# Gates of pairs 0 and 1 ahead of the branch, gelu low halves with routing between them, later w2 halves, block gathers at other places

## The chip, the cores and the metric

One core of a Trainium2 chip runs the whole program in one launch. The metric is the device time of that launch in microseconds. The kernel before was timed three times: 191.04, 191.51 and 192.29 us, median 191.51.

## The reference, cut to what matters

A small language-model tower on 4 x 512 tokens, width 128:

```python
h = take(W.T, x, axis=0)                              # token rows
n = layernorm(h)
s_t = tanh(s_{t-1} @ A.T + n_t @ B.T)                 # recurrence over 512 positions
y = einsum('bth,oh->bto', s, C)
h = h + (sigmoid(y @ Wg.T + bg) * y) @ Wo.T + bo
m = layernorm(h); logits = m @ gate_w.T               # top 1 of 8 experts, its weight is 1
moe = (silu(m @ w1[e].T) * (m @ w3[e].T)) @ w2[e].T   # e: the token's own expert
h = h + moe + gelu(m @ sw1.T) @ sw2.T                 # inner width 512
```

## The kernel before, in words

Tokens are 16 tiles of 128 rows. Five engine programs are written out by hand in order; semaphores alone order one engine against another. An engine never passes its own waiting instruction.

*Recurrence.* The 512 positions of 4 sequences are cut into 32 chunks of 16, and all chunks are run together as 128 columns: 40 warm-up steps and 16 real ones, `STEPS` = 56. Step i is two matmuls on PE (L457 input part, L459 state part, banks 0 and 1 by turns) and one tanh on ACT (L670). Beside it the tiles are gathered, normalised and turned (`turn_pair`, L444; `bring`, L663), and the weights are prepared: every f32 weight matrix is split into a scaled f16 high half and an f16 low half. ACT squares w3 and w2 pieces for their maxima (L680), PE turns and spreads the maxima (L466, L469 at `MAX_STEPS` and two steps behind), DVE makes powers of two of them, and from `HIGH_STEP` on ACT writes one high half of w3 or w2 per step (L690, L692). DVE writes the low halves (L920 for w1, L935 for w3 and w2; 512 columns each for the latter).

*Branch.* Five steps before the end DVE compares warmed-up states with those of the neighbouring chunk (L958 to L964) and writes `agree_i`. PE and ACT load it into a register and branch: if the chunks do not agree, the recurrence is done again position by position; on this data that body is skipped.

*Attention pairs.* A pair is two tiles, 256 columns of the last 16 steps' states. For pair n PE does gate(n) = wgc x states (L500) and c(n) (L520), ACT a tanh (L713), DVE `gated` (L975), PE wo (L529), DVE `attn_out` (L982), statistics and `shift`, POOL a power for the variance (L383), ACT `norm2` (L740), PE turns it (L538), ACT and DVE write its f16 halves `x_ffn` (L733, L999), and PE computes the logits (L545). All gates use bank 2, so gate(n) waits for tanh(n-1).

*Gelu stage.* The shared expert has 16 pieces n (4 groups of 4 tiles, times 4 slices of the inner width). PE `up(n)` (L510, 3 matmuls of 512 columns) into one of four banks; ACT gelu (L720), then the high half one piece behind (L725, function `shared`); DVE the low half (L1005, `act_low_half(n)`, semaphore `act_low`); `up(n)` waits for low half n-4. `down(m)` (L564, 12 matmuls of 128 columns) needs all four low halves of its group; after four of them DVE adds the group to `attn_out` (L1083, `take_down(g)`, semaphore `base_ready`), and SP stores it (L341). down of groups 2 and 3 waits for `base_ready` of the group two before. Between its low halves DVE computes the routing: counts, places, slots, one-hot lanes (L1060), and PE inverts the permutation with 16 small matmuls (L587) after down(`INVERT_AT`). DVE makes row indices of it (L1065 to L1076).

*Blocks.* Tokens are worked through in blocks of 128 rows of one expert, 20 on this data. POOL gathers a block's rows from `x_rows` (L395, `take_block(k)`), PE turns it (L600), ACT and DVE write its halves (L751, L1096 `turned_low`), PE w1 and w3 (L621), ACT silu (L760), DVE product (L1112), PE turns it (L634), halves (L767, L1125), PE w2 (L646), DVE output (L1120, L1138), POOL adds the rows to `out` in DRAM (L402). The first `AHEAD` = 13 gathers are written out ahead of the first add; the rest come between the adds.

## Time and profile before

| | |
|---|---|
| timed runs | 191.04, 191.51, 192.29 us |
| the profiled execution's own time | 191.32 us |
| its span in the trace | 189.5 us |
| busy: PE, DVE, ACT, POOL | 142.1, 129.6, 104.1, 81.1 us |
| mean granted clock of PE | 0.958 of full |

The span runs from the first to the last instruction in the trace; the profiled execution's time has 1.8 us more around it. A row of the timeline is a start, a duration, the engine, the line and the operation, with the tiles it writes and reads; in brackets stands how long the engine was idle before, and who released it. "issue" there means that the engine waited for nothing that the profile shows. A tile `w_sb` stands for several weight buffers, which are reused late in the program for other data (gelu low halves, gathered blocks, silu and products); `states` likewise holds the gelu high halves in the end. Line numbers are those of the kernel before.

### The profile page before, as it was taken

What the parts mean: (1) busy time and instruction counts of PE and PEld (TensorE: products, weight loads), DVE (VectorE), ACT (ScalarE), POOL (GpSimd) and SP (SyncE); (2) the same over time, 40 slices, a digit from 0 to 9 for tenths busy, and PEclk for the clock granted to TensorE, in tenths of its full rate; (3) what the DMA queues carried; (4) which work ended last, traced back from release to release, by engine and by line L of the source; (5) the groups of instructions that cost most, each with busy time, mean ns of one, the idle gap of its engine ahead of it and who ended that gap; (6) DMA issues with size and microseconds to landing.
All of it is one profiled execution on the core that took longest, in us unless ns stands there. A gap on an engine that the chain in (4) does not pass through costs nothing.

```text
span 189.5 us, 3241 instructions
## 1 busy us (share of the span) xinstructions
PE 142.1 (75%) x1001; PEld 100.7 (53%) x1001; DVE 129.6 (68%) x363; ACT 104.1 (55%) x239; POOL 81.1 (43%) x77
## 2 busy tenths in 40 slices
PE   0107977788888879886776986869999999999720
PEld 0106855566656557664324654854776666676510
DVE  0245767849778886898689782434878788887720
ACT  2002433799449973685997672317666566565400
POOL 4777855600000000334000076134488888887580
PEclk9999999999999999999697899699999999999995
DMA  5563346992000000111100013041023234343331
GB/s 150 176 180 99 108 143 195 338 386 103 0 0 0 3 0 3 40 74 55 55 3 0 0 42 109 5 166 58 28 37 53 31 44 43 39 37 40 28 31 14
DMA packets 9955, 13.83 MB, mean 73 GB/s; under 512 B 1936, under 2 KB 4752, under 8 KB 9936
## 3 DMA queue, kind: packets, MB, share of 16 engines
q1 hardware_dynamic: 5904, 9.91, 15.6%
q0 software_dynamic: 4032, 3.67, 12.4%
q8 instruction: 11, 0.18, 0.4%
q14 instruction: 8, 0.07, 0.1%
HBM read 10.17 MB, written 3.41 MB: 72 GB/s over the span
## 4 chain that ended last, share of the span: by engine, by line
PE 41%; ACT 18%; POOL 11%; DVE 10%; issue 9%; DMA 6%; SPq 1%; POOLq 0%; ACTq 0%; DVEq 0%
PE bank L621 13%; POOL emb_rows L351 8%; PE bank L646 7%; PE bank L564 7%; ACT attn_out L680 5%; PE bank L634 4%; PE bank L510 3%; ACT states L670 3%; DMA w_sb<-w 3%; ACT w_hl L690 3%; PE bank L459 2%; DMA emb_rows<-emb,tok_sb 2%; ACT bank L720 2%; ACT w_hl L692 2%; ACT states L725 2%
## 5 line engine op out<-in xcount | busy, mean ns | idle before, releaser
L402 POOL DMA_INDIRECT out<-out_blk,row_of x20 | 31.4, 1570 | 9.8 <-DVE out_blk L1138 5.6
L459 PE MATMUL bank<-states,sq_sb 128*128 128x128 f32 x112 | 27.3, 326 | 5.9 <-ACT states L670 1.0
L621 PE MATMUL bank<-w_hl,xblk_t 128*128 x120 | 29.2, 379 | 0.8 <-issue 0.8
L383 POOL TENSOR_TENSOR rstd<-vareps,cst 128x2 f32<-128x2 f32 x8 | 5.6, 697 | 47.8 <-DVE vareps L799 47.8
L459 PEld LDWEIGHTS bank<-states,sq_sb 128*128 128x128 f32 x112 | 17.4, 196 | 14.2 <-ACT states L670 13.4
L457 PE MATMUL bank<-x_in,sq_sb 128*128 128x128 f32 x112 | 23.4, 291 | 1.3 <-issue 0.7
L670 ACT ACTIVATE states<-bank 128x128 f32<-128x128 f32 x56 | 15.5, 276 | 13.4 <-PE bank L459 10.3
L395 POOL DMA_INDIRECT w_sb<-x_rows,row_in x16 | 15.4, 961 | 14.3 <-PE bank L600 7.2
L760 ACT ACTIVATE w_sb<-bank,factor 128x512 f32<-128x512 f32 x20 | 13.8, 688 | 13.4 <-PE bank L621 13.3
L457 PEld LDWEIGHTS bank<-x_in,sq_sb 128*128 128x128 f32 x112 | 17.9, 201 | 2.7 <-issue 1.9
L1112 DVE SCALAR_TENSOR_TENSOR w_sb<-bank,factor,w_sb 128x512 f32<-128x512 f32 x20 | 15.0, 749 | 5.9 <-ACT w_sb L760 4.7
L351 POOL DMA_INDIRECT emb_rows<-emb,tok_sb x16 | 15.6, 972 | 6.5 <-issue 4.3
L646 PE MATMUL bank<-w_hl,w_sb 128*128 x160 | 16.6, 246 | 2.2 <-DVE out_blk L1138 2.1
L510 PE MATMUL bank<-x_ffn,sw_hl 128*128 128x512 f16 x48 | 15.2, 438 | 3.7 <-DVE w_sb L1005 3.6
L621 PEld LDWEIGHTS bank<-w_hl,xblk_t 128*128 128x128 f16 x120 | 11.3, 98 | 11.3 <-issue 1.6
L1005 DVE SCALAR_TENSOR_TENSOR w_sb<-bank,factor,states 128x512 f16<-128x512 f32 x16 | 11.7, 744 | 7.1 <-ACT states L725 3.7
L564 PE MATMUL bank<-sw_hl,states 128*128 128x128 f16 x128 | 14.4, 240 | 2.0 <-issue 2.0
L720 ACT ACTIVATE bank<-bank,factor 128x512 f32<-128x512 f32 x16 | 10.7, 675 | 8.5 <-PE bank L510 6.7
L646 PEld LDWEIGHTS bank<-w_hl,w_sb 128*128 128x128 f16 x160 | 12.6, 98 | 4.3 <-issue 3.1
L767 ACT ACTIVATE w_sb<-bank 128x512 f16<-128x512 f32 x20 | 11.9, 597 | 4.1 <-PE bank L634 3.3
L1125 DVE TENSOR_TENSOR w_sb<-bank,w_sb 128x512 f16<-128x512 f32 x20 | 13.6, 681 | 0.5 <-ACT w_sb L767 0.5
L564 PEld LDWEIGHTS bank<-sw_hl,states 128*128 128x128 f16 x128 | 11.8, 110 | 3.7 <-issue 2.3
(144 smaller groups left out, 276.6 us busy)
## 6 DMA issues: line engine op xcount, KB each, us to landing
w_sb<-w SPq DMA_DIRECT2D x24, 256.0 KB, 6.1
x_rows<-norm SPq DMA_DIRECT2D x4, 256.0 KB, 2.4
out<-attn_out SPq DMA_DIRECT2D x4, 256.0 KB
sw_sb<-sw SPq DMA_DIRECT2D x2, 256.0 KB
cst<-consts SPq DMA_DIRECT2D x1, 420.0 KB
sq_sb<-sq SPq DMA_DIRECT2D x1, 384.0 KB
out<-out_blk,row_of POOLq DMA_INDIRECT x20
emb_rows<-emb,tok_sb POOLq DMA_INDIRECT x16
```

What stands on the lines that cost most here:

```text
L351: pool.indirect_dma_start(out=emb_rows[:, t, :], out_offset=None, in_=emb, in_offset=bass.IndirectOffsetOnAxis(ap=tok_sb[:, t:t + 1], axis=0),
L395: pool.indirect_dma_start(out=xblk(k), out_offset=None, in_=x_rows, in_offset=bass.IndirectOffsetOnAxis(ap=row_in[:, k:k + 1], axis=0),).t ...
L402: pool.indirect_dma_start(out=out, out_offset=bass.IndirectOffsetOnAxis(ap=row_of[:, k:k + 1], axis=0), in_=out_blk[k % RING][:], in_offse ...
L457: pe.matmul(by_batch(pre), bt, x_at[:, p, :, PADK - shift:XB - shift], start=True, stop=False)
L459: pe.matmul(pre, at, states[:, i * COLS:(i + 1) * COLS], start=False, stop=True).then_inc(pre_ready, 1)
L510: mm = pe.matmul(ups[n % UPS][:], sw1_hl[:, a, i * P:(i + 1) * P], x_ffn[:, b, g * GC:(g + 1) * GC], start=(j == 0), stop=(j == 2))
L564: mm = pe.matmul(bank[2 + g % 2][:, t * P:(t + 1) * P], (act_hi, act_lo)[a][:, g, i, t * P:(t + 1) * P], sw2_hl[:, b, i * P:(i + 1) * P], ...
L621: mm = pe.matmul(hb[:], xblk_t[:, k % 3, b * P:(b + 1) * P], w[:, bass.ds(e * INNER + a * EXPERTS * INNER, INNER)], start=(j == 0), stop=( ...
L646: mm = pe.matmul(bank[6][:, 0:width], (prod_hi, prod_lo)[a][:, u, i * P:(i + 1) * P], w[:, bass.ds(at_i, width)], start=(i == 0 and a == 0 ...
L670: act.activation(states[:, (i + 1) * COLS:(i + 2) * COLS], bank[i % 2][:, 0:COLS], ACT.Tanh).then_inc(state_ready, 1)
L720: act.activation(ups[n % UPS][:], ups[n % UPS][:], ACT.Gelu, scale=gelu_in).then_inc(gelu_done, 1)
L1112: dve.scalar_tensor_tensor(out=prod[:, u, :], in0=bank[2 + u][:], scalar=prod_scale, in1=silu[:, u, :], op0=ALU.mult, op1=ALU.mult).then_i ...
```

## The change

- `TURN_AT`: pairs 6 and 7 are turned after steps 11 and 13, before after 10 and 12. The second spread matmul moves from step 34 to 36 (`SPREAD_STEPS`), the high halves begin at step 38 instead of 39. The w1 high half is written in two pieces, the second behind the maxima; the low halves of w1 are cut 2, 2, 4 instead of 3, 3, 2.
- Gate(0) goes into the recurrence after step 53, gate(1) after step 54, in banks 2 and 3; their tanh follow tanh 54 on ACT, ahead of the branch. Step 55, the last, is moved behind the branch, and on PE behind c(0). If the branch is taken, the two gates are done again in it.
- Three of DVE's five w2 low halves that stood ahead of the pairs move behind `take_down(1)`, `(2)` and `(3)`. PE waits for the last of them (`w_split` 3) only before the first w2 matmuls.
- In the gelu stage DVE's low halves stand earlier among the routing; `take_down(0)` stands before low half 13; the inverse follows down(6), before down(2).
- POOL's gathers: 0 and 1 at once, 2 and 3 behind the last low half, 4 and 5 behind `base_ready` 2 and 3, 6 to 12 behind turned blocks 1, 2, 2, 3, 4, 4, 5. Before, 0 to 3 at once, 4 to 7 behind low halves 9, 11, 13, 15, and 8 to 12 behind turned blocks 1 to 5.

```diff
+TURN_AT = {0: 1, 2: 2, 4: 3, 6: 4, 8: 5, 11: 6, 13: 7}
+SPREAD_STEPS = (22, 36)
-HIGH_STEP = 39
+HIGH_STEP = 38
-INVERT_AT = 2
+TURNED_FIRST = (1, 2, 2, 3, 4, 4, 5)
+INVERT_AT = 6
+        gate_bank = lambda n: bank[3 if n == 1 else 2]
...
             for k in range(AHEAD):
-                if BESIDE <= k < BESIDE + 4:
-                    pool.wait_ge(act_low, 9 + 2 * (k - BESIDE))
-                elif k >= BESIDE + 4:
-                    pool.wait_ge(blk_turned, k - BESIDE - 3)
+                if k == 2:
+                    pool.wait_ge(act_low, GROUPS * IC)
+                elif k in (4, 5):
+                    pool.wait_ge(base_ready, k - 2)
+                elif k >= 6:
+                    pool.wait_ge(blk_turned, TURNED_FIRST[k - 6])
                 take_block(k)
...
+            def gate(n):
+                if n >= 2:
+                    pe.wait_ge(tanh_ready, n)
+                pe.matmul(gate_bank(n)[:, 0:PC], wgc[:], kept(n), start=True, stop=True).then_inc(wg_done, 1)
-                    if i == at_step + 2:
+                    if i == spread_step:
                         pe.wait_ge(diag_ready, b + 1)
...
                 if i == STEPS - 3:
                     pe.wait_ge(close_ready, 1)
-                    pe.transpose(bank[2][0:1, 0:P], close_row[:, 0:1], ident).then_inc(close_turned, 1)
+                    pe.transpose(bank[7][0:1, 0:P], close_row[:, 0:1], ident).then_inc(close_turned, 1)
+                    pe.wait_ge(wgc_ready, 1)
+                    gate(0)
                 if i == STEPS - 2:
+                    gate(1)
                     pe.wait_ge(agree_ready, 1)
...
-            gate(0)
             for s in range(PAIRS + 5):
                 if s < PAIRS:
                     n = s
+                    if n == 1:
+                        advance(STEPS - 1)
+                        pe.wait_ge(state_ready, 1 + STEPS)
+                        pe.wait_ge(sh_split, 3)
...
-                if s + 1 < PAIRS:
+                if 1 <= s and s + 1 < PAIRS:
                     gate(s + 1)
...
                 if i == STEPS - 2:
+                    act.wait_ge(bg_ready, 1)
+                    gate(0)
+                    gate(1)
                     act.wait_ge(agree_ready, 1)
...
+            advance(STEPS - 1)
...
-            for j in range(EXPERTS - 5, EXPERTS):
-                w2_low(j)
+            w2_low(EXPERTS - 5)
+            w2_low(EXPERTS - 4)
...
             for g in range(1, GROUPS):
                 take_down(g)
+                w2_low(EXPERTS - GROUPS + g)
```

PE at the branch, before: the end of step 53 and the first instructions of the pairs, with the body of the branch between them left out. L457 and L459 are a step, L473 turns the row of agreements, L476 loads the register.

```order
L459 MATMUL bank<-states,sq_sb 128x128 [waits state_ready]
L473 MATMUL bank<-cst,close_row 1x128 [waits close_ready]
L457 MATMUL bank<-x_in,sq_sb 128x128
L459 MATMUL bank<-states,sq_sb 128x128 [waits state_ready]
L476 TENSOR_LOAD agree_i [waits agree_ready]
L476 ISA x2
L457 MATMUL bank<-x_in,sq_sb 128x128
L459 MATMUL bank<-states,sq_sb 128x128 [waits state_ready]
L479 COMPARE_AND_BRANCH
```

Here the load stands between steps 54 and 55. The first after the branch, also before:

```order
L500 MATMUL bank<-states,wgc 128x256 [waits state_ready,sh_split,wgc_ready]
L520 MATMUL bank<-states,sq_sb 128x256
L500 MATMUL bank<-states,wgc 128x256 [waits tanh_ready]
L520 MATMUL bank<-states,sq_sb 128x256
L500 MATMUL bank<-states,wgc 128x256 [waits tanh_ready]
```

Gate(0) opens the pairs there. The same two places now (L465 and L467 are a step, L475 a gate, L492 the row of agreements, L498 the load, L538 c(n)):

```order
L467 MATMUL bank<-states,sq_sb 128x128 [waits state_ready]
L492 MATMUL bank<-cst,close_row 1x128 [waits close_ready]
L475 MATMUL bank<-states,wgc 128x256 [waits wgc_ready]
L465 MATMUL bank<-x_in,sq_sb 128x128
L467 MATMUL bank<-states,sq_sb 128x128 [waits state_ready]
L475 MATMUL bank<-states,wgc 128x256
L498 TENSOR_LOAD agree_i [waits agree_ready]
L498 ISA x2
L501 COMPARE_AND_BRANCH
```

Two gates stand in front of the load, and no step behind it. After the branch, on PE too:

```order
L538 MATMUL bank<-states,sq_sb 128x256 [waits state_ready]
L465 MATMUL bank<-x_in,sq_sb 128x128
L467 MATMUL bank<-states,sq_sb 128x128 [waits state_ready]
L538 MATMUL bank<-states,sq_sb 128x256 [waits sh_split,state_ready]
L475 MATMUL bank<-states,wgc 128x256 [waits tanh_ready]
```

Step 55 stands behind c(0), and gate(2) is the first gate left.

DVE in the second half of the gelu stage, before. L1005 is a low half, L1060 a half of the one-hot lanes, L1065 to L1076 the indices, L1083 `take_down`.

```order
L1060 TENSOR_TENSOR w_sb<-late,lane_i 128x1024
L1005 SCALAR_TENSOR_TENSOR w_sb<-bank,factor,states 128x512 [waits act_high]
L1060 TENSOR_TENSOR w_sb<-late,lane_i 128x1024
L1005 SCALAR_TENSOR_TENSOR w_sb<-bank,factor,states 128x512 [waits act_high]
L1065 TENSOR_SCALAR row_in<-bank 128x23 [waits inverse_done]
```

Low halves 6 and 7 stand beside the lanes, the indices follow. Behind the indices, on DVE before:

```order
L1005 SCALAR_TENSOR_TENSOR w_sb<-bank,factor,states 128x512 [waits act_high] x4
L1083 SCALAR_TENSOR_TENSOR attn_out<-bank,factor,attn_out 128x512 [waits down_done]
L1005 SCALAR_TENSOR_TENSOR w_sb<-bank,factor,states 128x512 [waits act_high] x4
L1083 SCALAR_TENSOR_TENSOR attn_out<-bank,factor,attn_out 128x512 [waits down_done] x3
L1096 TENSOR_TENSOR xblk_t<-bank,xblk_t 128x128 [waits xt_high] x2
```

Eight low halves are left there, three `take_down` in a row behind them.

Now (L1037 a low half, L1104 lanes, L1046 `take_down`, L967 a w2 low half, L1132 `turned_low`):

```order
L1104 TENSOR_TENSOR w_sb<-late,lane_i 128x1024
L1037 SCALAR_TENSOR_TENSOR w_sb<-bank,factor,states 128x512 [waits act_high] x2
L1104 TENSOR_TENSOR w_sb<-late,lane_i 128x1024
L1037 SCALAR_TENSOR_TENSOR w_sb<-bank,factor,states 128x512 [waits act_high] x2
L1046 SCALAR_TENSOR_TENSOR attn_out<-bank,factor,attn_out 128x512 [waits down_done]
L1037 SCALAR_TENSOR_TENSOR w_sb<-bank,factor,states 128x512 [waits act_high]
L1112 TENSOR_SCALAR row_in<-bank 128x23 [waits inverse_done]
```

Five low halves and `take_down(0)` have come in front of the indices. Behind the indices, now:

```order
L1037 SCALAR_TENSOR_TENSOR w_sb<-bank,factor,states 128x512 [waits act_high] x2
L1046 SCALAR_TENSOR_TENSOR attn_out<-bank,factor,attn_out 128x512 [waits down_done]
L967 SCALAR_TENSOR_TENSOR w_hl<-w_sb,scale_i,w_hl 128x4x128 [waits w_high]
L1046 SCALAR_TENSOR_TENSOR attn_out<-bank,factor,attn_out 128x512 [waits down_done]
L967 SCALAR_TENSOR_TENSOR w_hl<-w_sb,scale_i,w_hl 128x4x128 [waits w_high]
L1046 SCALAR_TENSOR_TENSOR attn_out<-bank,factor,attn_out 128x512 [waits down_done]
L967 SCALAR_TENSOR_TENSOR w_hl<-w_sb,scale_i,w_hl 128x4x128 [waits w_high]
L1132 TENSOR_TENSOR xblk_t<-bank,xblk_t 128x128 [waits xt_high] x2
```

Low halves 9 to 13 and `take_down(0)` stand ahead of the indices, which start with L1112 and, before, with L1065; only two low halves are left behind them, and each later `take_down` has a w2 half behind it.

## Rows read from the trace of the kernel before

**Rows 1.** The page's chain that ended last: shares of the span.

```profile
PE 41%; ACT 18%; POOL 11%; DVE 10%; issue 9%; DMA 6%; SPq 1%; POOLq 0%; ACTq 0%; DVEq 0%
```

**Rows 2.** Timeline, step 34: start us, us, engine, operation, [idle before <-releaser].

```profile
48.92 1.81 DVE L920 SCALAR_TENSOR_TENSOR w_hl<-w_sb,scale_i,w_hl 128x1536 f16<-128x1536 f32 x1
...
50.88 0.28 ACT L670 ACTIVATE states<-bank 128x128 f32<-128x128 f32 x1 [0.58 <-PE bank L459]
52.29 0.28 ACT L670 ACTIVATE states<-bank 128x128 f32<-128x128 f32 x1 [1.13 <-PE bank L459]
...
51.23 0.38 PE L469 MATMUL bank<-max_diag,cst 2*128 2x2 f32 x2 [0.39 <-DVE max_diag L868]
```

**Rows 3.** Timeline at the branch.

```profile
68.10 0.14 DVE L964 CAST agree_i<-agree 1x1 int32<-1x1 f32 x1
68.17 3.38 DVE L935 SCALAR_TENSOR_TENSOR w_hl<-w_sb,scale_i,w_hl 128x512 f16<-128x512 f32 x5
...
69.47 0.39 PE L459 MATMUL bank<-states,sq_sb 128*128 128x128 f32 x2
...
70.31 0.67 PE L500 MATMUL bank<-states,wgc 128*128 128x256 f32 x2 [0.46 <-ACT states L670]
```

**Rows 4.** The chain from 66 to 76 us: start us, us, what.

```profile
68.50 0.65 issue
...
71.08 0.48 ACT gate_t L713
...
74.05 0.43 DVE attn_out L982
```

**Rows 5.** DVE's timeline in the gelu stage.

```profile
103.41 1.22 DVE L1060 TENSOR_TENSOR w_sb<-late,lane_i 128x1024 f16<-128x1024 f32 x1
...
108.09 0.18 DVE L1065 TENSOR_SCALAR row_in<-bank 128x23 int32<-128x23 f32 x1 [1.00 <-PE bank L587]
...
109.37 2.05 DVE L1005 SCALAR_TENSOR_TENSOR w_sb<-bank,factor,states 128x512 f16<-128x512 f32 x3
112.31 0.75 DVE L1005 SCALAR_TENSOR_TENSOR w_sb<-bank,factor,states 128x512 f16<-128x512 f32 x1 [0.90 <-ACT states L725]
```

**Rows 6.** ACT's timeline, gelu 14.

```profile
116.31 0.66 ACT L720 ACTIVATE bank<-bank,factor 128x512 f32<-128x512 f32 x1 [2.71 <-PE bank L510]
```

**Rows 7.** The chain from 108 to 130, and the waits from 113 to 120.

```profile
113.61 0.67 PE bank L564 x12
...
119.14 6.58 PE bank L564 x86
...
PE bank L564 <- issue: 2.5, 4, 1.1
```

**Rows 8.** By stretches: us, each engine's busy (instructions), PEclk, DMA share, GB/s.

```profile
119.20:122.50 3.30, 3.30 (x32) 3.30 (x32) 1.96 (x3) 1.84 (x3) 0.94 (x1) 0.50 0.00 0
122.50:125.60 3.10, 3.10 (x57) 3.10 (x55) 0.86 (x2) 0.00 (x0) 0.00 (x0) 0.99 0.51 190
```

**Rows 9.** Timeline: POOL's gathers, first and last of seven; SP's stores.

```profile
109.07 1.02 POOL L395 DMA_INDIRECT xblk<-x_rows,row_in  x1 [19.43 <-DVE row_of L1068]
...
116.64 0.94 POOL L395 DMA_INDIRECT w_sb<-x_rows,row_in  x1 [0.30 <-issue]
...
113.75 13.11 SPq L341 DMA_DIRECT2D out<-attn_out  x4
```

**Rows 10.** ACT's timeline, the second square of w3.

```profile
35.45 0.63 ACT L680 ACTIVATE attn_out<-w_sb 128x512 f32<-128x512 f32 x1 [0.48 <-DMA w_sb<-w]
```

**Rows 11.** Timeline at the blocks' start; DMA view, a gather's landing.

```profile
125.75 0.75 DVE L1083 SCALAR_TENSOR_TENSOR attn_out<-bank,factor,attn_out 128x512 f32<-128x512 f32 x1 [1.93 <-PE bank L564]
...
127.96 1.28 ACT L760 ACT_TABLE_LOAD   x1 [0.51 <-issue]
...
w_sb<-x_rows,row_in POOLq DMA_INDIRECT x16, 2.7
```

**Rows 12.** DMA share, 60 to 76 us, tenths in 40 slices.

```profile
DMA  0000010000000000000000000000000100000000
```

More of the change, by code:

```diff
@@ L671, in _, with gate_tanh, gate @@
                                ).then_inc(state_ready, 1)
-                if i % PPP == 0 and i // PPP + 1 < PAIRS:
-                    bring(i // PPP + 1)
+            def gate_tanh(n):
+                return act.activation(gate_t[:, n % 2, :], gate_bank(n)[:, 0:PC], ACT.Tanh, bias=half_bg[:, 0:1], scale=0.5)
+            def gate(n):
+                act.wait_ge(wg_done, n + 1)
+                if n >= 2:
+                    act.wait_ge(gated_ready, n - 1)
+                gate_tanh(n).then_inc(tanh_ready, 1)
+            for i in range(STEPS - 1):
+                advance(i)
+                if i in TURN_AT:
+                    bring(TURN_AT[i])
                 j = i - SQUARE_STEP
@@ L1007, in act_low_half, with take_down @@
                                          ).then_inc(act_low, 1)
+            def take_down(g):
+                ts = slice(4 * g, 4 * g + 4)
+                dve.wait_ge(down_done, g + 1)
+                dve.scalar_tensor_tensor(out=attn_out[:, ts, :],
+                                         in0=bank[2 + g % 2][:].rearrange("q (t d) -> q t d", t=4),
+                                         scalar=base_unscale, in1=attn_out[:, ts, :], op0=ALU.mult, op1=ALU.add
+                                         ).then_inc(base_ready, 1)
             te = lambda ap: ap.rearrange("q (t e) -> q t e", e=EXPERTS)
@@ L1063, in _ @@
                 act_low_half(n)
+                act_low_half(n + 1)
+            take_down(0)
+            act_low_half(13)
             dve.wait_ge(inverse_done, 1)
@@ L1077, in _ @@
                               ).then_inc(experts_ready, 1)
[L1079 to L1089 removed]
+            for n in range(14, GROUPS * IC):
                 act_low_half(n)
[L1091 to L1092 removed]
             def turned_low(k):
```

86 lines of the change are left out of this document (40 added, 46 removed).

## The prediction

> **What bounds the kernel now.** I read the page first, then the chain of waits by window, the timeline engine by engine, and last the table by stretches. By the page the chain runs through every engine, PE with 41% of it [rows 1]: gathers, then 56 recurrence steps, the attention pairs, the gelu stage, and 20 expert blocks on PE. No engine bounds the whole, so the change has to be priced where its pieces stand. Four places matter.
>
> (a) Step 34 of the recurrence. Two tanh start 1.41 us apart, with 1.13 us of idle before the second where the one before had 0.58: PE's queue stood at the spread matmul (L469), which waited for DVE's max_diag [rows 2]. That is 0.55 us lost, on the chain.
>
> (b) The branch. DVE writes agree_i until 68.24; the chain shows 0.65 us of "issue" on PE (the register load), then step 55 and gate(0) at 70.31, its tanh at 71.08, and so on by turns of PE and ACT to attn_out of pair 0 at 74.05 [rows 3, 4]. Beside it DVE runs five w2 halves until 71.55 [rows 3]. The order of the later pairs is the same in both kernels.
>
> (c) The gelu stage. DVE works almost without a gap until it waits for the inverse: low halves of 0.75 us (0.67 apart when back to back) among the routing. The two lane pieces (1.22 each) and the 1.00 us wait for the inverse hold low halves 8 to 10 back until 109.37; low half 11 comes at 112.31 [rows 5].
>
> (d) A stall. ACT's gelu 14 starts at 116.31, 2.71 us after ACT went idle and the matmuls before it were over [rows 6]. PE, among matmuls that wait for nothing, shows "issue" 4 times, 2.5 us in all [rows 7], and its next 3.3 us run at a granted clock of 0.50, so at 1.2 and not 2.4 GHz [rows 8]. The stall begins when the first store of the base (SP, 113.75) joins the seven gathers of POOL, one each 1.25 us [rows 9]. The last 96 matmuls of the stage, at 0.67 a dozen, would take 5.4 us; they end 10.8 us after 114.9, where the last group with an up ends (113.61 + 0.67 + 0.65) [rows 7].
>
> **The change part by part**, in times of the trace of before.
>
> 1. *Spread at step 36, w1's high half in two pieces, high halves from step 38.* With a 1.2 us second high piece and a low piece of 1.2 (1.81 for 1536 columns [rows 2]) diag is ready near 51.9, before PE comes to step 36. The 0.55 of (a) goes. Scales come near 54.6 and tanh 38 ends there too, so ACT waits about 0.1. Worth 0.45. Turning pairs 6 and 7 a step later I cost at nothing: ACT waits for w3's transfer behind it (0.48 us at 35.45 [rows 10]), which sets the chain again. Without that cover it would be 0.1.
>
> 2. *Gates 0 and 1 ahead of the branch, step 55 behind c(0).* Gate(0) takes PE between 0.45 and its 0.67 busy [rows 3] in front of step 54 and makes that about 0.25 late. With part 1, tanh 54 falls near 68.3, gate(1) runs until 68.5, and the register load ends near 69.2. The branch then stands alone on PE. Before, it lay under tanh 55, between L459 at 69.47 and gate(0) at 70.31: at most 0.6, perhaps nothing [rows 3]. I take 0.4, since nothing is nearer to an end. c(0) begins near 69.6 and gated(0) near 70.2, DVE being free since 69.5 because three of its five w2 halves went. Then step 55, c(1), gate(2) and wo(0), so attn_out(0) near 72.55 against 74.05. Parts 1 and 2: **1.5 us**, carried through the pairs; bounds 0.9 (the branch at 0.6, gate(0) wholly late) to 2.0. Queued behind gate(0) on PE is only the recurrence; on ACT two tanh (0.48 each [rows 4]) stand before its own load, which holds back only tanh 55.
>
> 3. *Low halves as they come, inverse after down(6), take_down(0) before low half 13.* I walked DVE's new order with the rows' durations: low 2 ends near 98.0, low 6 at 102.9, low 8 at 105.3, low 10 at 107.7, low 12 at 110.3, take_down(0) at 111.0, low 13 at 111.7, the indices at 113.0, low 15 at 114.35, take_down(1) at 115.05. down(12) to (15) wait for base_ready 2, start there and end near **117.75**. The same walk with the old order and no stall gives low 13 at 115.5, low 15 at 117.5, take_down(1) at 118.2 and the end near **121.0**; the trace has 125.7. So the order is worth 3.2 and the stall costs 4.7. Bounds of the 3.2: nothing (DVE's work is the same, and a PE at half clock, as from 119.2 to 122.5 [rows 8], could give it back) to 4.0.
>
> 4. *Gathers.* By my walk they fall at 112.0, 113.3, 114.5, 115.7, 117.0, 118.2: still with stores, but held by events, not seven at one stretch. None is late: blocks come every 2.5 us, and a gather lands in 2.7 [rows 11]. How much of the stall is left no row tells. Its ends are no stall (4.7 gained; nearest row, 122.5 to 125.6, where stores move 190 GB/s and PE is busy for all 3.10 us [rows 8]) and all of it (0 gained; nearest row, the stall itself). The two are equally near, so I take the middle, **2.3**.
>
> 5. *Three w2 halves behind the take_downs.* Two fall into DVE's waits for down matmuls (1.93 us before the last take_down [rows 11]). The third stands between take_down(3) and turned_low(0). Behind turned_low(0) wait PE's second block turn, ACT's copy and the 1.28 us table load [rows 11], all on the chain, so it costs **0.67** (3.38 for five [rows 3]); bounds 0.6 to 0.75. The blocks behind are as before.
>
> Sum: 1.5 + 3.2 + 2.3 - 0.67 = 6.3 us. The profiled execution took 191.32 (span 189.5 and 1.8 around it), 0.2 below the median, so I forecast **185.0 us**.
>
> **The rivals.** A measurement of this kernel can tell about 1%, 1.9 us, from no change.
>
> *A, the stall vanishes*, chance 0.25. For: no stretch of seven gathers is left. 191.3 - 1.5 - 3.2 - 4.7 + 0.7 = 182.6; with part 2 at its best, 182.
>
> *B, the stall stays whole*, 0.17. For: three stores now fall beside gathers inside the stage. 187.3.
>
> *C, the branch costs more*, 0.05. Anything up to 0.6 us lay under tanh 55. The strip of DMA work from 60 to 76 has work only at 62.0 and 72.4 us, none between 69.5 and 70.3 [rows 12], so nothing was fetched at the branch; the body is longer now, and its end could lie further off. By that rule the sum would be 5.3 instead of 6.3; this trace passed the branch without it.
>
> *D, the order pays nothing and the stall stays*, 0.08. For: DVE's work is the same and the indices come 4 us later. 191.3 - 1.5 + 0.7 = 190.5, no change.
>
> *E, slower*, 0.05. If each store that meets gathers brings 4.7 us, there are three such meetings before the stage ends (stores 0, 1 and 2) where there was one: 191.3 + 9.4 - 4.0 = 196.7. It decides from two and a half stalls on. Against it: the later stores cost PE nothing in 122.5 to 125.6 [rows 8].
>
> The forecast itself (order pays, part of the stall goes) has 0.40. **Range** 181.5 to 189.0: A with a good part 2, the forecast with the order worth nothing (188.2), B and C; D and E are out. **Chances:** the forecast, A, B and C lie under 189.6 with 0.87, less 0.02 for their tails: faster 0.85. D and the tails give same 0.09, E and mishaps of its kind 0.06.
>
> **What would show it.** Right: tanh 0.86 us apart through steps 34 to 36; attn_out(0) near 72.5; the last take_down 6 to 10 us before 125.75; one w2 half between it and the first turned low half, and the blocks unchanged. Wrong: "issue" gaps of PE among the down matmuls while a store runs (B), at more than one store (E); a gap over 0.8 us between the load and c(0) (C); DVE idle in the gelu stage with ACT's high half as releaser, which says that the walk of part 3 was too short (D). The forecast fails upward altogether if the stall has nothing to do with gathers.

## The result and the profile after

| | before | after |
| --- | --- | --- |
| time, median (lowest to highest) | 191.53 us (191.04 to 192.29), 4 runs | 188.57 us (187.13 to 188.85), 4 runs |
| profiled execution | 191.32 | 188.85 |
| its span | 189.5 | 187.1 |

The ratio is 0.9875, 95% interval 0.9834 to 0.9916: 2.96 us faster by the medians, 2.47 by the two profiled executions. The forecast was 185.0 us, a gain of 6.3; the time lies in the range (181.5 to 189.0), the gain is less than half. A second set of runs on another chip gave 189.42 against 191.66, ratio 0.9892 (0.9761 to 1.0023). Ratios leave out executions more than 1.5% above the fastest of their kernel, and the traces of e3, e8, e11, e12 and g2 come from such executions, so only intervals are read from them.

One edit is missing from the list of the change above: the new kernel also moves `pool.drain()`, at which POOL is idle for some 2.5 us, from ahead of gather 8 to ahead of gather 6. It matters in e5 and h1 below.

The handovers of DVE that divide the time, first. They answer to [rows 4, 11]. Timeline of the kernel after: start us, us, engine, operation, [idle before <-releaser]; L1014 is attn_out of pair 0, L1064 onehot, L1046 take_down(0) to (3), L1149 prod(0) to prod(3).

```profile
71.82 0.43 DVE L1014 SCALAR_TENSOR_TENSOR attn_out<-bank,emb_rows 128x256 f32<-128x256 f32 x1 [0.38 <-PE bank L547]
...
92.07 0.38 DVE L1064 TENSOR_TENSOR onehot<-cst,first_rev 128x128 f32<-128x128 f32 x1
...
108.03 0.74 DVE L1046 SCALAR_TENSOR_TENSOR attn_out<-bank,factor,attn_out 128x512 f32<-128x512 f32 x1
...
111.94 0.73 DVE L1046 SCALAR_TENSOR_TENSOR attn_out<-bank,factor,attn_out 128x512 f32<-128x512 f32 x1
114.61 0.75 DVE L1046 SCALAR_TENSOR_TENSOR attn_out<-bank,factor,attn_out 128x512 f32<-128x512 f32 x1 [1.29 <-remote]
119.19 0.75 DVE L1046 SCALAR_TENSOR_TENSOR attn_out<-bank,factor,attn_out 128x512 f32<-128x512 f32 x1 [3.17 <-PE bank L582]
...
124.91 0.75 DVE L1149 SCALAR_TENSOR_TENSOR w_sb<-bank,factor,w_sb 128x512 f32<-128x512 f32 x1 [2.88 <-PE bank L639]
...
127.50 0.75 DVE L1149 SCALAR_TENSOR_TENSOR w_sb<-bank,factor,w_sb 128x512 f32<-128x512 f32 x1 [1.64 <-PE bank L639]
...
129.34 0.75 DVE L1149 SCALAR_TENSOR_TENSOR w_sb<-bank,factor,w_sb 128x512 f32<-128x512 f32 x1
...
133.10 0.74 DVE L1149 SCALAR_TENSOR_TENSOR w_sb<-bank,factor,w_sb 128x512 f32<-128x512 f32 x1
```

The last take_down stood at 125.75 [rows 11], so 6.56 us were won by there, almost all that was forecast (1.5 + 3.2 + 2.3 = 7.0). Then it melts: prod(0) was at 129.98 and is 5.07 earlier; prod(3) was at 135.72 and is 2.62 earlier. From prod(3) on the blocks run as before, and 2.4 of the 2.6 reach the end of the span.

The chain of waits of the kernel after (start us, us, what) shows the two holes. It answers to [rows 7].

```profile
112.81 1.72 PE bank L582 x28
...
115.01 0.28 issue
115.29 0.45 PE bank L582 x5
115.75 0.29 issue
...
117.53 1.64 PE bank L582
...
119.94 0.66 DVE w_hl L967
...
122.06 2.74 PE bank L639 x6
...
125.02 2.37 PE bank L639 x6
...
130.29 1.66 another core or an unknown queue
```

From 112.81 the last 48 down matmuls are free of waits (2.85 us, as later runs show); they come in handfuls with gaps between, and DVE hears of their end at 119.19. At 130.29 a second hole begins, 1.66 long, in which DVE waits for a matmul (L1157, the read of y) whose signal is late. "Unknown queue" and "remote" are the profile's words where the engine named by the wait had long been done.

The stretches of the kernel after (us, busy time by engine with instructions, PEclk, DMA share, GB/s) answer to [rows 8]:

```profile
117.80:122.00 4.20, 0.51 (x2) 0.18 (x1) 1.87 (x4) 0.56 (x3) 1.40 (x3) 0.79 0.24 83
122.00:127.90 5.90, 5.84 (x19) 2.72 (x20) 1.38 (x4) 3.20 (x5) 2.79 (x4) 0.57 0.17 47
127.90:134.00 6.10, 4.95 (x39) 3.35 (x36) 4.21 (x10) 3.50 (x7) 2.70 (x3) 1.00 0.12 33
```

From the end of block 0's turn (117.86) to step 0 (122.06) PE has only block 1's turn to do; the granted clock falls to about half, so 1.2 and not 2.4 GHz, and the six matmuls of steps 0 and 1 take 2.74 and 2.37 us instead of 1.29. Before, the half clock lay inside the stall [rows 8], and the first blocks ran at full.

POOL's gathers after, first two and last of the six in the stage (timeline); they answer to [rows 9]:

```profile
110.32 1.02 POOL L401 DMA_INDIRECT xblk<-x_rows,row_in  x1 [22.91 <-DVE row_of L1115]
111.65 0.95 POOL L401 DMA_INDIRECT xblk<-x_rows,row_in  x1 [0.30 <-issue]
...
117.14 0.94 POOL L401 DMA_INDIRECT w_sb<-x_rows,row_in  x1 [0.31 <-issue]
```

They were to be spread, but their events come as fast as POOL issues: still one each 1.25 to 1.55 us. Three more follow at 120.58 to 123.08, one at 125.29, three at 127.77 to 130.27.

No instruction is loaded beside the first hole: from 115.0 to 119.2 us the DMA view of either kernel has packets of q0 (software_dynamic, POOL's) and q1 (hardware_dynamic, SP's) alone, none of the instruction queues q8 and q14.

### The profile page after: what moved, and what is told of

It reads as the page before. It is cut to its first block, busy times and chain, and to the rows that moved or that the text cites. A ratio compares the mean times of both kernels' runs of the same rounds, so it can differ in the third digit from the quotient of the medians.

```text
span 187.1 us, 3243 instructions
## 1 busy us (share of the span) xinstructions
PE 141.2 (75%) x1001; PEld 99.6 (53%) x1001; DVE 129.0 (69%) x364; ACT 103.7 (55%) x239; POOL 81.6 (44%) x77
## 4 chain that ended last, share of the span: by engine, by line
PE 39%; DVE 15%; ACT 14%; POOL 12%; issue 8%; DMA 7%; SPq 2%; another core or an unknown queue 1%; POOLq 0%
PE bank L639 14%; POOL emb_rows L357 8%; PE bank L666 7%; PE bank L582 4%; DMA w_sb<-w 4%; ACT attn_out L713 4%; PE bank L652 4%; DVE w_sb L1037 3%; PE bank L525 3%; ACT states L690 3%; ACT w_hl L723 3%; PE bank L467 2%; ACT w_hl L725 2%; DMA emb_rows<-emb,tok_sb 2%; SPq L340 2%
## 5 line engine op out<-in xcount | busy, mean ns | idle before, releaser
L639 PE MATMUL bank<-w_hl,xblk_t 128*128 x120 | 31.6, 403 | 0.9 <-issue 0.9
L467 PE MATMUL bank<-states,sq_sb 128*128 128x128 f32 x112 | 27.4, 328 | 6.3 <-ACT states L690 1.4
L467 PEld LDWEIGHTS bank<-states,sq_sb 128*128 128x128 f32 x112 | 17.6, 198 | 14.8 <-ACT states L690 14.1
L465 PE MATMUL bank<-x_in,sq_sb 128*128 128x128 f32 x112 | 23.6, 294 | 1.6 <-ACT x_in L683 1.5
L1149 DVE SCALAR_TENSOR_TENSOR w_sb<-bank,factor,w_sb 128x512 f32<-128x512 f32 x20 | 15.0, 750 | 7.6 <-PE bank L639 4.5
L465 PEld LDWEIGHTS bank<-x_in,sq_sb 128*128 128x128 f32 x112 | 18.3, 203 | 2.7 <-ACT x_in L683 1.6
L666 PE MATMUL bank<-w_hl,w_sb 128*128 x160 | 17.1, 251 | 3.2 <-DVE out_blk L1175 3.2
L525 PE MATMUL bank<-x_ffn,sw_hl 128*128 128x512 f16 x48 | 14.0, 411 | 1.9 <-DVE w_sb L1037 1.7
L401 POOL DMA_INDIRECT xblk<-x_rows,row_in x4 | 4.2, 1040 | 23.8 <-DVE row_of L1115 22.9
L582 PE MATMUL bank<-sw_hl,states 128*128 128x128 f16 x128 | 12.2, 219 | 1.1 <-issue 0.6
L781 ACT ACTIVATE xblk_t<-bank 128x128 f16<-128x128 f32 x20 | 5.5, 276 | 12.5 <-PE bank L618 11.5
L1157 DVE TENSOR_SCALAR out_part<-bank,factor 128x128 f32<-128x128 f32 x20 | 7.0, 351 | 7.6 <-PE bank L666 4.7
```

Source lines behind the costliest of these rows:

```text
L401: pool.indirect_dma_start(out=xblk(k), out_offset=None, in_=x_rows, in_offset=bass.IndirectOffsetOnAxis(ap=row_in[:, k:k + 1], axis=0),).t ...
L465: pe.matmul(by_batch(pre), bt, x_at[:, p, :, PADK - shift:XB - shift], start=True, stop=False)
L467: pe.matmul(pre, at, states[:, i * COLS:(i + 1) * COLS], start=False, stop=True).then_inc(pre_ready, 1)
L525: mm = pe.matmul(ups[n % UPS][:], sw1_hl[:, a, i * P:(i + 1) * P], x_ffn[:, b, g * GC:(g + 1) * GC], start=(j == 0), stop=(j == 2))
L582: mm = pe.matmul(bank[2 + g % 2][:, t * P:(t + 1) * P], (act_hi, act_lo)[a][:, g, i, t * P:(t + 1) * P], sw2_hl[:, b, i * P:(i + 1) * P], ...
L639: mm = pe.matmul(hb[:], xblk_t[:, k % 3, b * P:(b + 1) * P], w[:, bass.ds(e * INNER + a * EXPERTS * INNER, INNER)], start=(j == 0), stop=( ...
```

## Experiments

Eighteen runs on five chips. On four of them the kernel before takes about 191 us (190.9, 190.9, 191.7, 191.0); on the third, called chip C here, 186.7. Ratios are to the kernel before on the same chip. The theory grew in steps: first stores against gathers, then gathers alone, then the form in which they are issued.

### Stores, gathers, or both (first chip)

e1: SP's base stores wait for the last take_down.

```
-                sp.wait_ge(base_ready, g + 1)
+                sp.wait_ge(base_ready, GROUPS)
```

> The changed kernel, but SP issues all four base stores only after the last take_down; the gathers stay where they are. In the changed kernel the last take_down starts at 119.19, where down(12) to (15), begun at 112.81 and 2.7 us long at full clock, should have let it start near 115.6. Theory S (the stores, alone or beside gathers, hold PE up): the last take_down starts near 115.6, no issue gaps among the down matmuls, steps 0 and 1 of the blocks at full clock, time 188.6 - 3.6 - 2.5 = about 182.5 us. Theory G (gathers alone hold PE up): stall as before, 188 to 189. Theory N (neither; the dense stream of down matmuls holds itself up): stall as before, 188 to 189.

Measured: 189.1 us, ratio 0.9913 (0.9871 to 0.9956). The chain of e1, where the stores are issued only at 121.81:

```profile
115.00 1.36 another core or an unknown queue
...
116.39 0.75 DVE attn_out L1046
...
117.80 3.21 another core or an unknown queue
```

The stall is the same (1.36 and 3.21 us ahead of take_down(2) and (3)) with not one base store under way. The stores are acquitted, and with them half of my part 4.

e2: gathers 2 to 5 of POOL wait for the last take_down instead. e3: stores and gathers both.

```
                 if k == 2:
-                    pool.wait_ge(act_low, GROUPS * IC)
-                elif k in (4, 5):
-                    pool.wait_ge(base_ready, k - 2)
+                    pool.wait_ge(base_ready, GROUPS)
```

> The changed kernel, but gathers 2 to 5 wait for the last take_down; the stores stay, and gathers 0 and 1 still fall ahead of the stall's beginning. Theory G, and also the form of S in which only a store beside a gather does harm: no stall, last take_down near 115.6, about 182.5 to 184 us. Theory S in the form that stores alone do it, and theory N: stall as before, 188 to 190. Gathers 2 to 5 come late enough to hold no block up if one gather takes 1.25 us to issue and 2.7 to land.

> Both of the two edits: neither a store nor gathers 2 to 5 before the last take_down. Theories S and G: last take_down near 115.6, about 182.5 us. Theory N: the stall stays although no transfer runs, 188 to 189. If stores and gathers now collide at the start of the blocks, the stall turns up there instead, between the last take_down and block 3, and the time is 185 to 188.

Measured: e2 193.44 us, ratio 1.0137 (1.0109 to 1.0164); e3 194.68, ratio 1.0164 (1.0098 to 1.0231). The chain of e2:

```profile
112.46 2.85 PE bank L580 x48
115.34 0.75 DVE attn_out L1044
...
130.65 2.10 issue
...
133.51 7.20 issue
```

The stage is clean: 48 down matmuls in 2.85 us. The stall has moved with the gathers and grown: seven of them, 1.25 us apart from 124.82 to 132.32, stand beside a hole of 9.3 us in all. The second part outlasts the run and ends at 140.71, when POOL issues adds and gathers by turns. So moving the run moves the stall. e3, whose four stores are issued from 117.93 to 119.73, shows the same: 2.40 us between its last two take_downs, then seven gathers 1.25 us apart from 126.48 and a first hole of 4.99 us at 128.71.

e4: w2's last low half behind turned_low(1) (part 5).

```
             turned_low(1)
+            w2_low(EXPERTS - 1)
```

> The changed kernel, with the w2 low half that stands between take_down(3) and the first turned low half moved behind the second. By the prediction's part 5 that half costs 0.67 us on the chain: 0.67 less than the changed kernel, ratio to before about 0.984 instead of 0.9875. Rival: the wait for PE's late matmuls or the clock that falls afterwards sets the start of the blocks, and the time does not move by more than 0.2.

Measured: 189.44 us (187.03 to 190.84), too wide to tell. From the last take_down to prod(0) its trace has 4.83 us where the kernel after has 5.72; both have the half clock there (2.74 us for the six matmuls of step 0), so the 0.67 of part 5 is neither shown nor refuted.

### What in the gathers (second chip)

e5: the old waits of the gathers in the new kernel, and the drain ahead of gather 8 again, so eight in a row.

```
-DRAIN_AT = 6
+DRAIN_AT = 8
...
-                if k == 2: ... elif k >= 6: ...
+                if BESIDE <= k < BESIDE + 4:
+                    pool.wait_ge(act_low, 9 + 2 * (k - BESIDE))
+                elif k >= BESIDE + 4:
+                    pool.wait_ge(blk_turned, k - BESIDE - 3)
```

> The changed kernel with the gathers of the kernel before (0 to 3 at once, 4 to 7 by low halves, 8 to 12 by turned blocks 1 to 5). Theory B (a long run of gathers, one right behind the other, makes all engines see each other's signals late, from about the fourth gather on): eight gathers in one run from 110.3 to 120, the stall among the down matmuls is as long as in the changed kernel or longer, the last take_down starts at 119 to 122, and the start of the blocks is free of a second one; time 187.5 to 191. Theory P (the place of the gathers changes nothing): 188.6 within 0.5.

Measured: 190.46 us, ratio 0.9947 (0.9905 to 0.9988). Its last take_down comes behind a hole of 5.91 us at 116.14, 7.35 us behind take_down(2), where the kernel after has 4.58. From onehot to the last take_down e5 has 29.88 us, the kernel after 27.12, so in the stage the new places of the gathers are worth 2.8 us; but e5 has no second hole (prod(2) to prod(3) 2.50 us, not 3.76). In the time 1.4 us is left (0.9947 against 0.9875, from two chips, with intervals that touch).

e7: 40 ACT copies of one column in ACT's idle stretch, against the thought that many small instructions or their records slow the signals.

```
+            for c in range(40):
+                act.activation(gate_t[:, 0, c:c + 1], half_bg[:, 0:1], ACT.Copy)
```

> The changed kernel with 40 more ACT copies of one column in the stretch where ACT is idle, between its last gelu high half and its first block. Theory R (what holds PE up is the number of instructions that all engines together carry out and record): the stall grows, the last take_down starts a microsecond or more later, time 190 or more. Theory B (the run of gathers does it): the last take_down starts where it did, 119.2, time 188.6 within 0.7, unless the copies themselves are still running when the first block is turned.

Measured: 189.99 us, ratio 0.9999 (0.9957 to 1.0041), above what was expected, and I can't explain it; but from take_down(1) to the last the trace has 7.19 us (113.20 to 120.39), the kernel after 7.25. By this one trace the stall is not made longer.

e8: gathers 2 to 5 at one event each, 11 blocks ahead (`AHEAD` 13 to 11, and later events for the gathers from 6 on).

```
-                elif k in (4, 5):
-                    pool.wait_ge(base_ready, k - 2)
+                elif k in (3, 4):
+                    pool.wait_ge(base_ready, k - 1)
+                elif k == 5:
+                    pool.wait_ge(base_ready, GROUPS)
```

> The changed kernel with gathers at single events: 0 and 1 at once, 2 behind the last low half, 3 and 4 behind base_ready 2 and 3, 5 behind base_ready 4, 6 to 10 behind turned blocks 2 to 5, and only 11 of them ahead of the first add (13 before). No run is longer than 3 or 4. Theory B: the stall shrinks to under a microsecond, the last take_down starts near 115.6 to 117 and no stall at 130; time 183 to 186. Rival: POOL's queue binds instead, since nine gathers stand between adds at 3.2 us a block against PE's 2.5; then blocks 8 to 14 come 3.2 us apart and the time is 186 to 189. Theory P: 188.6.

Measured: 188.75 us, ratio 0.9858 (0.9769 to 0.9947). The gathers still stood 1.3 to 1.5 us apart, five of them; take_down(1) to the last is 5.85 us and not 7.25. The second hole, which was to go, stayed (1.69 us at 130.40, beside gathers at 127.88, 129.13 and 130.38), and POOL fell behind the blocks late in the run: at 167.78 DVE has waited 2.07 us for an add, and prod(16) comes 4.47 us behind prod(15).

e9: all 20 block gathers become plain transfers of 128 rows in order on SP, at the same events; the permutation is left out, the bytes are the same.

```
-                take_block(k)                      # POOL, indirect
+                sp.dma_start(xblk(k), x_rows[k % TILES * P:(k % TILES + 1) * P, :])
```

> The changed kernel with the 20 block gathers of POOL replaced by plain transfers that SP issues at the same events: block k gets 128 rows of the normalised tokens in their order, 64 KB as before, so the permutation is left out. POOL issues only the adds. Theory B in the form that POOL's indirect transfers do the harm: no stall, last take_down near 115.6, blocks at 2.5 us, time 180 to 183. If the traffic itself does the harm, whoever issues it: stall as in the changed kernel, 187 to 189.

Measured: **180.84 us**, ratio 0.9466 (0.9377 to 0.9556). Its chain:

```profile
113.79 2.85 PE bank L597 x48
116.65 0.03 issue
116.67 0.75 DVE attn_out L1061
...
119.55 1.47 PE bank L654 x6
...
121.12 1.29 PE bank L654 x6
```

Neither hole is there, and the clock holds. Same bytes, same buffers, same stores: so many bytes in flight are not what stalls. Two things changed together here, the engine that issues and the form, and the rows are read in order and not scattered.

### Form, number, drain, order (chip C)

e10: POOL keeps the 20 loads, at the same places, as plain transfers (permutation left out). e11: blocks 2 to 5 alone on SP (permutation left out for them). e12: a drain of POOL ahead of each gather. e13: part 3 undone.

```
e10 -                pool.indirect_dma_start(out=xblk(k), ..., in_offset=...row_in[:, k:k + 1]...)
    +                pool.dma_start(xblk(k), x_rows[k % TILES * P:(k % TILES + 1) * P, :])
e11 -                if k == 2: ...
    +                if k in (2, 3, 4, 5):
    +                    continue                   # SP loads them
e12 -                if k == DRAIN_AT:
    +                if k >= 1:
                         pool.drain()
e13 -INVERT_AT = 6
    +INVERT_AT = 2     # and DVE's low halves and take_down(0) where they stood before
```

> The changed kernel; the 20 block gathers stay on POOL, at the same places of its queue and behind the same waits, but are plain transfers of 128 rows in order, without a table of indices (the permutation is left out). Theory B (it is the indirect form, in runs of several, that holds up the handovers of all engines): no stall among the down matmuls, last take_down near 116.5, time near that of the kernel with the loads on SP, 181 to 182.5. Rival P (any transfer that POOL issues in such a run does it, since each is made ready by POOL itself): the stall stays whole, last take_down 119 to 120, 188 to 189.

> The changed kernel; block gathers 2 to 5 alone are plain transfers of rows in order on SP (the permutation is left out for these four blocks); POOL gathers blocks 0 and 1 as before and then nothing until block 6 behind turned block 1. Theory B with a run's length as its dose: the first stall (3.6 us) and the half clock behind it (2.5) go, the three gathers 6 to 8 are too few to bring one, and the one at 130 (1.7) goes too or stays small: 181.5 to 184. Rival Q (the number of gathers does not matter, each that meets a handover delays it): the gathers at 120 to 130 bring stalls of their own, 185 or more.

> The changed kernel with a drain of POOL ahead of each block gather from 1 on, not of gather 6 alone; everything that it computes is unchanged. If the stall comes of gathers issued back to back, so that POOL's work for one is still queued behind the next, the drains spread them or bound the queue: last take_down 115.5 to 117.5, 183 to 186. If it comes of their rate or their mere number, the pitch stays 1.25 us and so does the stall: 188 to 189.

> The changed kernel with part 3 undone: DVE's order of low halves, routing and take_down(0) is that of the kernel before, and the inverse stands behind down(2) again; the gathers keep the changed waits (block 2 behind the last low half). Prediction's part 3: the order is worth 3.2 us, so take_down(1) comes at 115.2 to 116.3 instead of 112, and the time is 190 to 192 if the stall stays where the gathers are. Rival D (the order pays nothing, the stall takes it back): 188 to 189.5, the last take_down at 119 to 120 as with the new order.

Measured: e10 181.98 us, ratio 0.9799 (0.9712 to 0.9886); e11 183.39; e12 207.99, ratio 1.1152 (1.1052 to 1.1251); e13 186.47, ratio 0.9988 (0.9942 to 1.0035). e11 (180.53 to 184.35) is too wide for a ratio. e12 is plain: at each drain POOL is idle for 2.3 to 2.9 us where it is 0.3 without, the gathers stand 3.2 to 3.8 apart, and the blocks wait for them. The surprise was e13. POOL and DVE in its timeline:

```profile
114.65 0.94 POOL L401 DMA_INDIRECT xblk<-x_rows,row_in  x1 [6.59 <-DVE w_sb L1037]
115.90 0.95 POOL L401 DMA_INDIRECT xblk<-x_rows,row_in  x1 [0.30 <-issue]
117.15 0.94 POOL L401 DMA_INDIRECT w_sb<-x_rows,row_in  x1 [0.30 <-issue]
...
114.30 0.74 DVE L1046 SCALAR_TENSOR_TENSOR attn_out<-bank,factor,attn_out 128x512 f32<-128x512 f32 x1
115.62 0.75 DVE L1046 SCALAR_TENSOR_TENSOR attn_out<-bank,factor,attn_out 128x512 f32<-128x512 f32 x1
118.07 0.75 DVE L1046 SCALAR_TENSOR_TENSOR attn_out<-bank,factor,attn_out 128x512 f32<-128x512 f32 x1 [1.04 <-PE bank L582]
```

Indirect gathers in a row, then seven more from 122.62 to 130.11, and no stall at all. e11 has none either: beside its gathers at 124.34 to 126.84 prod(3) comes 2.50 us behind prod(2). Either the old order protects, or chip C does. So the same kernels had to run elsewhere.

### The same kernels on a fourth chip

> The changed kernel itself once more, with a profile. If the stall belongs to some chips (theory K), then where the kernel before takes about 187 this one has no stall beside the gathers, last take_down about 3.8 us after take_down(1), and takes 182.5 to 184; where the kernel before takes about 191 the stall is there, 7.2 us between the two, and it takes 187 to 189. If it belongs to the order of the work (theory O), the stall is there on either chip, and the time 187 to 189 on both.

> The changed kernel with part 3 undone, once more. Theory K: where the kernel before takes about 191, a stall of 3 to 4 us appears beside gathers 2 to 12 and the time is 190 to 192; where it takes 187 there is none and the time is 186 to 187. Theory O: no stall on either chip.

> POOL's block gathers as plain transfers (permutation left out), once more. On a chip with the stall: 181 to 182.5 if only the indirect form brings it, 185 or more if any transfer of POOL does. On a chip without: 181 to 182.5 in any case, as before.

> Blocks 2 to 5 by plain transfers of SP (permutation left out for these), once more. On a chip with the stall: no stall of the down matmuls, and a stall of 1 to 4 us from the fourth of the seven gathers 6 to 12 on, near 122 to 130 us, so 184 to 187, if a run of gathers brings it. On a chip without: 181 to 184, as before.

Measured: g1 189.42 us, ratio 0.9892; g2 191.59, 0.9952 (0.9897 to 1.0008); g3 **182.78**, 0.9587 (0.9481 to 0.9692); g4 184.80, 0.9634 (0.9524 to 0.9744). The trace of g1 has both holes again: 4.67 us between the last two take_downs, 1.78 us of idle time on DVE ahead of 131.41. DVE in the timeline of g2, the kernel of e13 (its onehot stands 3.8 us later than there, so compare intervals):

```profile
120.02 0.74 DVE L1046 SCALAR_TENSOR_TENSOR attn_out<-bank,factor,attn_out 128x512 f32<-128x512 f32 x1
124.99 0.75 DVE L1046 SCALAR_TENSOR_TENSOR attn_out<-bank,factor,attn_out 128x512 f32<-128x512 f32 x1 [3.56 <-remote]
```

2.45 us between the last two take_downs on chip C, 4.97 here. The stall belongs to the chip, not to the order: theory K. The times say the same: the kernels with indirect gathers that ran on both chips differ by some 5 us (before 191.7 and 186.7, the old order 191.6 and 186.5), the plain one by 0.8 (182.78 and 181.98). And on this chip, which stalls, DVE in the timeline of g3 (POOL issues, but plainly):

```profile
113.03 0.73 DVE L1044 SCALAR_TENSOR_TENSOR attn_out<-bank,factor,attn_out 128x512 f32<-128x512 f32 x1
115.46 0.75 DVE L1044 SCALAR_TENSOR_TENSOR attn_out<-bank,factor,attn_out 128x512 f32<-128x512 f32 x1 [1.05 <-PE bank L580]
...
121.19 0.75 DVE L1147 SCALAR_TENSOR_TENSOR w_sb<-bank,factor,w_sb 128x512 f32<-128x512 f32 x1 [3.03 <-PE bank L637]
```

No stall. POOL's plain transfers are harmless here; its indirect ones are not. Both forms use the same queue with the same packets and bytes, as the DMA views of the kernel after and of g3 show (packets, MB, share of 16 engines):

```profile
q0 software_dynamic: 4032, 3.67, 12.6%
```

```profile
q0 software_dynamic: 4032, 3.67, 13.0%
```

What in the form does it is not separated. A plain transfer holds POOL for 0.53 us and an indirect one for 0.94, so no run of plain ones was as long (three, 1.58 us, is the longest), and the rows of the plain ones lie in order. g4 shows it piece by piece: without gathers 2 to 5 the stage is clean (2.38 us between the last two take_downs), while the second hole stays, 1.75 us at 126.75, beside the gathers of blocks 9 to 12; e11, the same kernel on chip C, doesn't have it.

g3 also isolates the clock. Stretches of g3, then of e10, the same kernel on chip C, both from the start of step 0:

```profile
118.30:121.20 2.90, 2.86 (x8) 1.23 (x9) 0.01 (x1) 1.78 (x2) 1.57 (x3) 0.50 0.26 72
```

```profile
118.46:121.35 2.89, 2.88 (x14) 1.25 (x14) 0.95 (x2) 2.54 (x4) 1.97 (x4) 1.00 0.23 72
```

Half clock in the one, full in the other, after the same three microseconds in which PE has two block turns to do (2.8 from the end of the first to step 0). It needs no stall, and it doesn't always come. Of the nine traces with a clean stage and w2's last half ahead of the blocks, five (e11, e12, e13, g3, g4) have the half clock in steps 0 and 1, four (e2, e3, e9, e10) don't; of the eight with a stall at the end of the stage (after, g1, g2, e1, e4, e5, e7, e8) all have it.

### Two at most, and PE kept busy (fifth chip)

h1: gathers 2 to 11 held by single later events, 12 ahead (`AHEAD` 13 to 12), and e4's edit. h2: the same and 8 unread matmuls ahead of step 0.

```
h1  +                if k in (2, 3):
    +                    pool.wait_ge(base_ready, k + 1)
    +                elif k >= 4:
    +                    pool.wait_ge(blk_turned, TURNED_FIRST[k - 4])   # 2, 3, 3, 4, 4, 5, 5, 6
h2  +            keep_busy(5)      # between turn_block(0) and turn_block(1)
    +            keep_busy(3)      # behind turn_block(1)
```

> The changed kernel with block gathers 2 to 11 held by single events, so that at most two stand 1.25 us apart, and then POOL is free for a microsecond or more; 12 blocks ahead and not 13; w2's last low half behind the first two turned blocks. All is computed. On a chip where the kernel before takes about 191: if only a run of three or more stalls the others, both stalls (3.6 and 1.7 us) go and 0.5 comes from the low half: 182 to 184.5, ratio 0.955 to 0.967, last take_down 3.7 to 4.2 us after take_down(1). If each gather costs its part, wherever it stands: 187 or more, ratio above 0.975. On a chip that shows no stall: ratio about 0.98, and this tells nothing.

> The same with 8 matmuls of 128x512 (0.22 us each at full clock) whose result nobody reads: five between the turns of blocks 0 and 1 and three behind. If the idle stretch of PE ahead of the first block sets the half clock of steps 0 and 1 (2.7 us for six matmuls and not 1.29), they run at 1.29 to 1.6 and the time falls by 1 to 2.5 us against the kernel without them. If the clock falls whatever PE does there, it is the same time or up to 0.5 us more.

Measured: h1 190.37 us, ratio 0.9961 (0.9925 to 0.9997); h2 190.33, ratio 0.9950 (0.9923 to 0.9976). POOL in h1's timeline, and what DVE then waits:

```profile
120.19 0.94 POOL L401 DMA_INDIRECT w_sb<-x_rows,row_in  x1 [0.32 <-issue]
123.80 0.94 POOL L401 DMA_INDIRECT w_sb<-x_rows,row_in  x1 [2.67 <-issue]
...
130.06 0.94 POOL L401 DMA_INDIRECT w_sb<-x_rows,row_in  x1 [0.31 <-issue]
...
133.02 0.35 DVE L1157 TENSOR_SCALAR out_part<-bank,factor 128x128 f32<-128x128 f32 x1 [5.73 <-remote]
```

The expectation failed, and shows why. In the stage, where gathers stood apart, there is no stall (2.44 us between the last two take_downs). But the one drain ahead of gather 6, which I left in, held POOL for 2.67 us; its events had all come by then, and six gathers went out in a row from 123.80 to 130.06. The hole that I removed came back there as 5.7 us. Step 0 ran at full clock in h1 already, so h2 tells nothing of the clock. In both, w2's last half stands behind the turns, and 1.9 us lie between the end of block 0's turn and step 0 in h1, not 2.8.

Where the stall shows, by length of run on the four chips that have it:

| gathers in a row | late signals |
| --- | --- |
| 3 | none (after, 120.58; h1, 117.38), 1.7 (after, 127.77), 1.7 to 1.8 (e1, e8, g1, g4), 2.5 (e4, 126.70) |
| 4 | none (e2, 116.36), 2.5 (g2: 4.97 less 2.45) |
| 5 | 2.1 (e8: 25.75 less 23.64) |
| 6 | 3.5 (after), 5.7 (h1) |
| 7 | 5.0 (before), 9.3 (e2, 124.82) |
| 8 | 6.2 (e5: 29.88 less 23.64) |

The 23.64 is the clean length from onehot to the last take_down, from the next section. Indirect transfers back to back are not enough by themselves. In the kernel after, from 134.03 to 157.97 us, POOL issues adds and gathers by turns with 0.3 us between, so that a gather comes only each 3.2 us; the products come 2.39 to 2.64 us apart, about the 2.50 of the runs without a stall.

## Why the forecast was right in most steps and wrong in its sum

Take the clean lengths from the runs without a stall. From onehot to the last take_down the old order takes 26.44 us (e13: 91.63 to 118.07), the new one 23.64 (e10: 91.94 to 115.58); before took 31.45 (94.30 to 125.75), after 27.12. From the last take_down to prod(0) e10 takes 4.67, from prod(0) to prod(3) 5.74, as before did.

| step | forecast | measured | from |
| --- | --- | --- | --- |
| 1, 2: spread, gates ahead | +1.5 | +2.23 | attn_out(0) 74.05 to 71.82, onehot the same |
| 3: order of the low halves | +3.2 | +2.80 | 26.44 less 23.64 |
| 4: stall, in the stage | +2.3 | +1.53 | 5.01 before, 3.48 after |
| 5: w2's last half | -0.67 | -0.44 | 4.67 less 4.23 |
| half clock in steps 0 and 1 | 0 | -2.24 | 1.05 by prod(0), 1.19 more by prod(2) |
| second stall | 0 | -1.26 | prod(2) to prod(3) 3.76, not 2.50 |
| sum by prod(3) | +6.33 | +2.62 | 135.72 less 133.10 |

Steps 1 and 2 were too cautious. Tanh of step 34 to 36 come 0.85 and 0.85 apart as forecast. Part 2 put the register load (0.7 us) behind gate(1) and the branch (0.4) behind the load, so that c(0) would begin near 69.6. In the trace gate(1) ends at 68.31 and c(0) begins at 68.70: load and branch together leave 0.39 us of "issue", since `agree_i` was written by 67.49, before gate(1) began (67.88), so that most of the load seems to have run beside the gate. attn_out(0) at 71.82 and not 72.55 is the result. Rival C didn't come. The Trainium skill ("Runtime: NRT & Kernel Launch", Instruction fetch mechanics) would have a taken branch to an unfetched page wait; this trace shows 0.39 us and no instruction transfer there (the next one comes near 70.1). Step 3 was well read: the walk gave take_down(1) at 115.05 less the gain ahead of it, 112.8, and it came at 111.94. The walk's clean ends, 121.0 and 117.75, are near what the clean lengths give from before's onehot at 94.30: 120.74 and 117.94. D is refuted by e13 and e10; e12, whose gathers are indirect as in e13, also has 23.65 us. E did not come; by e1 the base stores have no part in the stall.

Step 4 was the wrong mechanism. I had a store joining gathers; it is gathers alone. With that the middle of two ends was no estimate: my walk had put the events 1.2 us apart, the pitch at which POOL issues anyway, so "held by events" spread nothing. B's time (187.3) came nearest, for other reasons.

The step that failed the sum is the last clause of part 5, "The blocks behind are as before". It put the clock and the second stall at nothing, without a reason, and they cost 3.50 of the 3.71 us that are missing. 1.26 are a stall beside the gathers from 127.77 on. 2.24 are half clock: PE's idle stretch now lies directly ahead of the blocks and not inside the stage. How much of the 2.24 is owed to the stall stays open, since g3 and e13 have the half clock without one; w2's half, which part 5 put there, lengthens that stretch too (2.8 us from block 0's turn to step 0 in g3 and e10, 1.9 in h1 and before), and nothing separates the two. The other steps nearly cancel: +0.73, -0.40, -0.77 and +0.23.

What stays open. Why POOL's indirect issue delays signals between other engines and opens gaps in PE's stream, and why one chip of five shows nothing of it. Whether scattered rows or POOL's longer work per transfer matter. Why the half clock comes in g3 and not in e10 or e9. How long a run may be: three and four go both ways. The changed kernel itself was not run on chip C; e13's 186.47 us there less the 2.8 us of the order put it near 183.7, an estimate. No version with all of its work done beats the changed kernel by more than can be measured (e8 0.9858 against 0.9875). e9 and g3 say what is to be had, 6 to 8 us, if the rows of a block could be fetched without POOL's indirect form.

## What to carry over

When signals between engines come late without a cause in the trace, lay the issue times of every other queue beside them, and test by the form of the suspect (who issues, plain or indirect) rather than by its place: moving it only moves the hole. A forecast that removes idle time must say where the next idle time will lie and what clock follows it. And check the chip before the kernel: two kernels compared on different chips differed here by more than the change.

## What the runs showed of the hardware

- On four chips a run of POOL's indirect gathers, one each 1.25 us, goes with late signals between PE, ACT and DVE and with gaps among matmuls that wait for nothing, 1.3 to 7.2 us at a time; a gather lands in 2.6 us all the while. The same transfers issued plainly by SP (e9) or by POOL (g3) don't.
- Not every run does it: three and four gathers go both ways, and a gather each 3.2 us between adds does nothing (the kernel after, 134 to 158 us).
- One chip of five does not show this (e11, e13); there the kernel before takes 186.7 us and not 191.
- With a drain between gathers POOL is idle 2.3 to 2.9 us and not 0.3 (e12); a plain transfer of 128 rows takes POOL 0.53 us in the stage (g3), an indirect one 0.94.
- After about 3 us with two block turns in them PE was granted 0.50 in one run (g3) and 1.00 in another (e10) of the same kernel.
